# Four hand-written orders of turns, changed in the first stage and in layers 2 and 3

## The chip, the cores and the metric

The kernel runs on one core of one Trainium2 chip. Its time is the device time of one execution in microseconds (us), the median of several runs. The profile adds one more execution, taken by the hardware profiler.

The engines of the core work side by side, each through its own list of instructions in order: TensorE (PE; its weight loads are PEld) multiplies matrices and transposes, VectorE (DVE), ScalarE (ACT) and GpSimd (POOL) do elementwise work, and SyncE (SP) issues the transfers. They meet only through semaphores: an instruction that waits holds up everything behind it on its own engine.

## The reference, cut to what matters

Four layers run on 4 elements of 1024 rows of 128 numbers. Each layer normalises, scales and shifts its input by a row of a modulation, applies a sequence operation, adds it back through a gate, normalises again and applies a feed-forward.

```python
mod = (_silu(L0_c) @ L0_wmod).reshape(L0_c.shape[0], 6, 1, -1)
h = _layernorm(x, axis=-1) * (1 + ca) + sa
x = x + ga * _L0_attn_ref(h, ...)      # relu features, state decayed by gamma, divided by a sum
h = _layernorm(x, axis=-1) * (1 + cb) + sb
x = x + gb * _L0_ffn_ref(h, ...)       # 8 experts, the best 2 of each row
...                                     # layer 1: four small transformer blocks, then 8 experts
...                                     # layer 2: a chunked delta rule, see below
...                                     # layer 3: a gated delta rule along 512 rows
```

The sequence operation of layer 2 needs the inverse of a unit triangular matrix for each chunk and then runs a recurrence over the chunks:

```python
A = solve_triangular(M, jnp.broadcast_to(eye, M.shape), lower=True, unit_diagonal=True)
v = A @ v
k_cumdecay = A @ (k_beta * decay_exp)
def step(S, inp):
    k_i, v_i, kcd_i = inp
    attn = jnp.tril(jnp.einsum('bhid,bhjd->bhij', k_i, k_i) * L[None])
    v_new = v_i - kcd_i @ S
    o_i = k_i * de @ S + attn @ v_new
    S_new = chunk_total_decay * S + jnp.einsum('bhcd,bhce->bhde', k_i * dw, v_new)
```

Layer 3 is of the same family: queries, keys, values, two sigmoids and a gate, a state that is updated at every row, and then a feed-forward of one expert for each part of the batch. The kernel computes it in chunks too, with an inverse and a recurrence.

## The kernel before, in words

Every one of the 4 elements has its own space (`room[b]`, tensor `arena`) and its own two banks of PSUM; small constants lie in `sm`, `cst`, `cols` and `rows`.

For each engine and each element there is a generator: `element_pe`, `element_act`, `element_dve` and `element_pool`, with one more, `common_...`, for what belongs to no element (the decay tables, the biases, the fold of weights). A generator issues the instructions of its engine for its element, layer by layer: `l0_...` and `mods_...`, `moe0_...`, `fold_...`, `l1_...`, `moe1_...`, `l2_...`, `l2f_...`, `l3_...`, `l3f_...`. It yields at many places. What it issues between two yields is here called a turn: often some four matmuls and their waits, one normalisation, or one group of GpSimd's operations. Some turns issue nothing.

Which generator moves next is written out by hand in the dict `TURNS`: a long string of digits for each engine. A digit 0 to 3 gives a turn to that element, 4 to the common part:

```python
parts = [element(b) for b in range(B)] + [common()]
for b in TURNS[h.name]:
    step(parts[int(b)])
for part in parts:
    while step(part):
        pass
```

The strings therefore set how the elements' work is interleaved on each engine, and nothing else. Within one element each engine's order is always the same. Which instruction waits for which is also always the same, with one exception: an element's products alternate between its two banks (`Banks.take`), and a product waits until the reader of that bank has freed it.

SyncE has no string. Its queue is written out in `queue_first` and the functions after it. It loads the inputs, the first weights, then waits in `queue_mods(0)` for the marks "shift" and "gates", that is for VectorE's last step of the first modulation, writes the modulation to DRAM and reads it back for each element (`kept`). Behind that wait stand the small weights, the constants, the experts' weights, the long row `rows` (2253 KB), the fold and the projections of layer 1; two more waits, for "bias3" and "fold", stand before the weights `wf1`, `wf2` and the modulations of layers 2 and 3.

The first stage: `common_act` copies the modulation rows and takes the sigmoid of the decay, `common_dve` makes the decay tables (a scan), adds 1 to the gates and later prepares the biases with `bias_middle` and eight memsets. For each element GpSimd and VectorE take the statistics of the rows (BATCH_NORM_STATS2), ScalarE normalises, TensorE transposes, ScalarE shifts by the modulation while it evicts the bank, and TensorE makes q, k and v; ScalarE applies relu to q and k.

Layer 2 and layer 3: seven rounds of two halves build the inverse on TensorE (`inv_pe`; turns `inv_f` and `inv_p`, the second of which transposes), with evictions by ScalarE and VectorE (`inv_act`, `inv_dve`), and with GpSimd, which shifts, masks and scales columns (`inv_pool`, `shift_pool`, `unit_pool`). The recurrence follows (`d2v` makes the new values, `d2s` the state; `r3...` in layer 3). It passes from TensorE to VectorE or ScalarE and back in each of its steps.

Lines that every operation comes through, and by which the profile names it: L87 matmul, L90 transpose, L98 and L99 ScalarE's activation, L104 elementwise on two tensors, L107 with a scalar, L110 scalar and tensor, L113 copy, L116 memset, L130 and L133 statistics, L136 reciprocal, L147 reduction, L152 a transfer.

## The time and the profile before

| | us |
|---|---|
| median of 3 runs | 1735.24 (1734.53 to 1736.05) |
| profiled execution, its own time | 1735.68 |
| its span, first to last instruction | 1733.9 |
| TensorE busy | 1698.8 (98%) |
| TensorE's weight loads, beside it | 1302.2 (75%) |
| VectorE busy | 1235.9 (71%) |
| GpSimd busy | 1218.6 (70%) |
| ScalarE busy | 1089.0 (63%) |
| number of instructions | 31801 |

Times in the trace run from the start of the span. A row of a timeline gives the start, the duration, the engine and line, the operation with what it writes and reads, and in brackets how long the engine was idle before it and which engine's operation released it. Neighbouring operations of a kind are joined in one row (x4). The granted clock of TensorE is 1.00 of full speed nearly everywhere, so the clock plays no part. In the page's 40 slices TensorE is at 9 tenths or more in all but the first and the last.

### The profile page before, as it was taken

Reading aid. Unit: us, or ns where it says so; the run is one execution under the profiler, and the core shown is the slowest. Engines: PE = TensorE matmul, PEld = TensorE weight load, DVE = VectorE, ACT = ScalarE, POOL = GpSimd, SP = SyncE. Lnnn points to the kernel's source line nnn. Section 1 sums busy time; section 2 is a strip of 40 time slices with the busy share of each in tenths; the row PEclk is TensorE's granted clock in tenths of the full one; section 3 lists DMA queues with packets and bytes.
Section 4 is the critical chain, followed back from the end, with each engine's and each line's share of the span. In section 5 each row is a group of like instructions: output and inputs, shape, how many; then the busy total and the mean of one; then the engine's idle time right before and its main releaser. Section 6 shows DMA issues by size and latency. Waiting matters only on the chain.

```text
span 1733.9 us, 31801 instructions
## 1 busy us (share of the span) xinstructions
PE 1698.8 (98%) x10006; PEld 1302.2 (75%) x10006; DVE 1235.9 (71%) x4490; ACT 1089.0 (63%) x2904; POOL 1218.6 (70%) x1771
## 2 busy tenths in 40 slices
PE   8999999999999999999999999999999899999998
PEld 5888888876667676676676777767788787788976
DVE  7954335688977988988899866445566766578773
ACT  6555226456677678777777886546546666665656
POOL 5655549898878987888799785135347876666667
PEclk9999999999999999999999999999999999999999
DMA  7100000010000000000000000000000001000002
GB/s 254 68 32 1 1 1 4 3 51 1 1 1 1 1 1 1 1 1 1 1 1 1 1 11 6 1 1 7 2 3 3 1 18 31 21 2 1 2 3 73
DMA packets 24027, 26.70 MB, mean 15 GB/s; under 512 B 3492, under 2 KB 20772, under 8 KB 23476
## 3 DMA queue, kind: packets, MB, share of 16 engines
q1 hardware_dynamic: 23860, 24.67, 4.6%
q8 instruction: 81, 1.33, 0.3%
q14 instruction: 86, 0.70, 0.1%
HBM read 22.52 MB, written 2.15 MB: 14 GB/s over the span
## 4 chain that ended last, share of the span: by engine, by line
PE 84%; DVE 5%; POOL 5%; ACT 4%; issue 2%; POOLq 0%; DVEq 0%; ACTq 0%
PE ps L87 77%; PE ps L90 7%; POOL arena L104 5%; ACT arena L98 3%; DVE arena L104 2%; DVE arena L110 1%; DVE arena L147 1%; DVE arena L130 0%; ACT arena L99 0%; ACT L98 0%; DVE arena L133 0%; DVE arena L107 0%; DVE arena L136 0%; DVE ps L147 0%; DVE ps L104 0%
## 5 line engine op out<-in xcount | busy, mean ns | idle before, releaser
L104 POOL TENSOR_TENSOR arena<-arena 128x512 f32<-128x512 f32 (+6 forms) x836 | 715.4, 869 | 277.7 <-DVE arena L110 96.5
L98 ACT ACTIVATE arena<-ps 128x128 f32<-128x128 f32 (+11 forms) x1204 | 338.8, 326 | 393.5 <-PE ps L87 285.2
L87 PE MATMUL ps<-arena 128*128 128x128 f32 (+4 forms) x2792 | 440.5, 291 | 9.1 <-DVE arena L104 3.8
L87 PEld LDWEIGHTS ps<-arena 128*128 128x128 f32 x2792 | 373.4, 192 | 96.0 <-issue 47.6
L104 DVE TENSOR_TENSOR arena<-ps,arena 128x128 f32<-128x128 f32 (+4 forms) x696 | 313.2, 469 | 175.7 <-PE ps L87 163.4
L98 ACT ACTIVATE arena<-arena 128x128 f32<-128x128 f32 (+1 forms) x836 | 321.2, 439 | 50.9 <-POOL arena L104 38.9
L87 PE MATMUL ps<-arena,moe 128*128 128x256 f32 (+1 forms) x960 | 288.2, 439 | 0.0
L87 PE MATMUL ps<-arena,cst 128*128 128x504 f32 (+2 forms) x768 | 283.8, 489 | 2.4 <-ACT arena L98 1.3
L98 ACT ACTIVATE arena<-ps,cols 128x512 f32<-128x512 f32 x324 | 216.8, 688 | 103.2 <-PE ps L87 96.3
L104 POOL TENSOR_TENSOR arena<-arena,cst 128x144 f32<-128x144 f32 (+7 forms) x536 | 186.2, 356 | 92.4 <-ACT arena L98 57.7
L110 DVE SCALAR_TENSOR_TENSOR arena<-ps,arena 128x128 f32<-128x128 f32 (+1 forms) x476 | 157.0, 365 | 119.6 <-PE ps L87 94.1
L90 PE MATMUL ps<-cst,arena 128*128 128x128 f32 (+1 forms) x1296 | 231.4, 274 | 8.6 <-ACT arena L98 6.0
L87 PEld LDWEIGHTS ps<-moe,arena 128*128 128x128 f32 x1728 | 202.2, 192 | 21.7 <-issue 15.0
L104 POOL TENSOR_TENSOR arena<-arena,mhalf 128x4 f32<-128x4 f32 (+1 forms) x140 | 150.3, 1074 | 93.7 <-DVE arena L147 89.5
L87 PEld LDWEIGHTS ps<-arena,moe 128*128 128x128 f32 x960 | 172.7, 191 | 50.9 <-issue 25.0
L90 PEld LDWEIGHTS ps<-cst,arena 128*128 128x128 f32 (+1 forms) x1296 | 157.7, 142 | 67.0 <-issue 24.6
L87 PE MATMUL ps<-moe,arena 128*128 128x128 f32 x1728 | 204.8, 276 | 0.1
L87 PEld LDWEIGHTS ps<-arena,cst 128*128 128x128 f32 x768 | 133.1, 190 | 78.3 <-issue 38.6
L147 DVE TENSOR_REDUCE arena<-arena 128x4 f32<-128x8 f32 (+3 forms) x368 | 180.2, 519 | 16.2 <-POOL arena L104 10.6
L104 POOL TENSOR_TENSOR arena<-arena,rows 128x512 f32<-128x512 f32 (+1 forms) x132 | 141.3, 1072 | 24.4 <-PE ps L90 15.8
L130 DVE BATCH_NORM_STATS2 arena<-arena 128x6 f32<-128x128 f32 x544 | 141.7, 275 | 20.9 <-POOL arena L104 12.8
L87 PE MATMUL ps<-arena,wf 128*128 128x512 f32 x256 | 127.8, 597 | 0.5 <-ACT arena L98 0.4
(120 smaller groups left out, 1761.9 us busy)
## 6 DMA issues: line engine op xcount, KB each, us to landing
rows<-in_rows SPq DMA_DIRECT2D x1, 2253.0 KB, 14.5
arena<-in_x SPq DMA_DIRECT2D x8, 256.0 KB, 5.2
wf<-in_wf SPq DMA_DIRECT2D x2, 1024.0 KB, 7.0
arena<-in_L_ffn_W SPq DMA_DIRECT2D x8, 256.0 KB, 3.0
out_dram<-arena SPq DMA_DIRECT2D x8, 256.0 KB, 2.7
wmod<-in_wmod SPq DMA_DIRECT2D x4, 384.0 KB, 8.1
arena<-kept SPq DMA_DIRECT2D x24, 64.0 KB, 3.0
arena<-kept SPq DMA_DIRECT2D x8, 192.0 KB, 3.2
```

What stands on the lines that cost most here:

```text
L87: return UNSENT if self.e is None else self.e.matmul(out, lhsT, rhs, start=start, stop=stop)
L90: return UNSENT if self.e is None else self.e.transpose(out, in_, ident)
L98: return self.e.activation(out, in_, func, bias=bias, scale=scale)
L104: return UNSENT if self.e is None else self.e.tensor_tensor(out, a, c, op)
L110: return UNSENT if self.e is None else self.e.scalar_tensor_tensor(out, a, s, c, op0, op1)
L130: return UNSENT if self.e is None else self.e.bn_stats(out, a)
L147: return self.e.tensor_reduce(out, a, AX.X, ALU.add, negate=negate)
```

## The change

Only the four strings in `TURNS` change. No function, no instruction, no wait and no buffer is added or taken away; every engine issues what it issued before, in another order.

```diff
--- before.py
+++ after.py
@@ -389,113 +389,113 @@
 TURNS = {
-    "pe": ("2000000000000120002230001222000112200011100211012003013211003031110332001332322330320113213131222121"
-          "1333222011133020000112103211133320042330100300213103322000203332002200300100003001200100032022202021"
-          "0011000230032021022113112213312210002232011011312222110311031101122101101011221210112122011311311221"
...
-          "0122321322331234313231223232000020230232331113111031333120002121120221332023311133231010322033320002"
-          "220333312232322223333133000110211"),
-    "dve": ("4000000000000000440111424242222222001122222230011133303233401000031221110020200113121003111000422202"
-           "3300133330211001112000003131211321300000121111032000033233321212230033331142102122000030030032330120"
-           "0000100011133232223231112110000101102113222000000333330112121320113333210123331221213311101110324211"
...
-           "1111111111111111232112301120032031222222222222222322011000311311113222233323333333333333334411330330"
-           "2222222312330333333213211000200033012141132240201333322233231"),
-    "act": ("4040400040220211222221111030110333333430112204000331000010100010203200210333012020011020222002320200"
...
-           "333222023030220132002220013213333033211023311"),
-    "pool": ("2041004201200302200102003031110011132200403312210012103330202231023133121132033111122133000000012223"
...
-            "10333221102033234012321001133221223233331000111223112122233000132333330011223200"),
+    "pe": ("0400000000002023000212020012200101210001210201021130110031000211130333200132312302333232113123121110"
+          "2233322201113022000111300321314332120013030300330210300032103322200220030010000330012001100020222020"
+          "2001100023003202100221133112213122100223201101131222211031103110112210110101122112011212201131131122"
...
+          "2132321323133231232223000020232203331011310131131332220221102103130113331023023113202233302233223322"
+          "330"),
+    "dve": ("4000000000001440202121200030211244222222132410332022103213012112001000211100010301400213004033321030"
+          "0003223313221131102102201000113110000101131310002320013313233222230303331210242003201120030330030000"
+          "0210100011132331224221312121230020110110132010030000321313230133330123011231313121113302222110311131"
...
+          "1101111111112112323122101130103222222222212222220233101010312013111022323332333333333333332223331032"
+          "1213220333333323232000332213231"),
+    "act": ("0420144400002022212121011100303333334211123203000001300410101200030022201033301020011100222200232020"
...
+          "003332222203331"),
+    "pool": ("4200301422100001200200310100132202110230431332011000233101220323011213111322301313301122000402003213"
...
+          "02031130220331221001223131223233331100001232122333"),
```

In all each string is 30 digits shorter (3333 to 3303 for TensorE, 3861 to 3831 for VectorE, 2145 to 2115 for ScalarE, 1180 to 1150 for GpSimd). Those 30 are turns that issue nothing, and with them the strings between look different in places although they give the same order. Read through the generators, so that only turns that issue something are counted (number 0 is the first), this is what changes:

| engine | working turns | changed at the start | changed behind |
|---|---|---|---|
| TensorE | 2753 | 15 to 114 (53 moved) | 1873 to 2748 (571 moved, by at most 11) |
| VectorE | 3322 | 12 to 252 (190 moved, by at most 18) | 2471 to 3320 (573 moved, by at most 18) |
| ScalarE | 1840 | 1 to 54 (20 moved) | 1301 to 1835 (350 moved, by at most 9) |
| GpSimd | 1030 | 0 to 64 (45 moved) | 715 to 1014 (150 moved, by at most 6) |

TensorE's working turn 115 starts at 92 us in the trace of before, its turn 1873 at 1323.6 us. Behind 1323 us lie layer 2, its feed-forward, layer 3 and its feed-forward, with the four elements interleaved and somewhat apart.

Some of the moves, with the number of the working turn before and after:

- ScalarE: the normalisations of element 0's first half 2 to 1, the first modulation row's copy 1 to 2, the sigmoid of the decay 7 to 4, the second copy of the biases 36 to 44.
- VectorE: the modulation's gates 26 to 42, its step for the shift 22 to 31, the statistics of elements 1, 2 and 3 to places ahead of element 0's last ones, element 0's second half 34 to 44, the decay table of layer 2 55 to 73, the block with `bias_middle` and the memsets 145 to 148, a step of element 1's recurrence 149 to 154.
- TensorE in layer 2: element 3's inverse, round 1, 1957 to 1960 and 1963 to 1966, its round 2 1964 to 1968 and 1971 to 1975, element 1's `d2v` 1982 to 1986, element 0's `d2s` 1991 to 1995, element 3's round 5 stays at 1999.
- TensorE in the last feed-forward: element 1's `f3wo` 2719 to 2722. The last turns of all engines stay as they are.

## Rows read from the trace of the kernel before

**Rows 1.** The page: its span, and the busy time of each engine.
```profile
span 1733.9 us, 31801 instructions
...
PE 1698.8 (98%) x10006; PEld 1302.2 (75%) x10006; DVE 1235.9 (71%) x4490; ACT 1089.0 (63%) x2904; POOL 1218.6 (70%) x1771
```

**Rows 2.** The page: the chain that ended last, by engine.
```profile
PE 84%; DVE 5%; POOL 5%; ACT 4%; issue 2%; POOLq 0%; DVEq 0%; ACTq 0%
```

**Rows 3.** Stretches: length; PE, PEld, DVE, ACT, POOL busy (records); clock; DMA; GB/s.
```profile
0.00:20.00 20.00, 15.50 (x40) 6.66 (x40) 10.79 (x65) 10.06 (x21) 7.64 (x24) 1.00 0.66 161
20.00:92.00 72.00, 70.37 (x473) 57.22 (x474) 64.52 (x336) 40.87 (x68) 47.11 (x71) 1.00 0.41 158
92.00:1323.00 1231.00, 1223.39 (x6672) 907.33 (x6671) 876.20 (x3019) 778.74 (x1922) 873.30 (x1006) 1.00 0.02 4
1323.00:1342.00 19.00, 18.76 (x162) 18.18 (x161) 15.55 (x57) 12.37 (x54) 16.55 (x43) 1.00 0.02 6
1342.00:1372.00 30.00, 25.71 (x199) 22.86 (x198) 21.01 (x67) 18.54 (x83) 25.98 (x71) 1.00 0.00 1
1372.00:1405.00 33.00, 31.38 (x249) 28.02 (x248) 24.27 (x87) 23.38 (x94) 29.08 (x82) 1.00 0.07 19
1405.00:1600.00 195.00, 191.30 (x1353) 159.98 (x1352) 136.40 (x526) 123.64 (x427) 129.23 (x297) 1.00 0.05 13
1600.00:1667.00 67.00, 66.27 (x514) 59.70 (x513) 50.19 (x171) 39.76 (x158) 42.23 (x123) 1.00 0.01 1
1667.00:1691.00 24.00, 19.45 (x132) 15.32 (x131) 20.71 (x116) 15.65 (x38) 16.04 (x30) 1.00 0.03 7
1691.00:1728.50 37.50, 36.36 (x225) 26.86 (x226) 15.56 (x54) 26.03 (x45) 31.44 (x28) 1.00 0.23 61
```

**Rows 4.** Timeline of ScalarE, 5 to 24 us: start, duration, operation.
```profile
9.87 1.63 ACT L98 ACTIVATE arena<-arena 128x128 f32<-128x128 f32 x4
...
16.43 1.28 ACT L98 ACT_TABLE_LOAD   x1
17.73 0.20 ACT L98 ACTIVATE gd<-rows 128x1 f32<-128x1 f32 x1
```

**Rows 5.** Timeline of TensorE, 5 to 23 us.
```profile
11.60 1.09 PE L90 MATMUL ps<-cst,arena 128*128 128x128 f32 x4 [0.87 <-ACT arena L98]
...
18.56 0.49 PE L87 MATMUL ps<-w,arena 128*128 128x128 f32 x2 [0.68 <-ACT arena L98]
```

**Rows 6.** Timeline of VectorE, 48 to 60 us: its longest operation there.
```profile
52.44 1.75 DVE L104 TENSOR_TENSOR wf<-wf,rows 64x1536 f32<-64x1536 f32 x1
```

**Rows 7.** Timeline of TensorE, 55 to 59 us.
```profile
57.40 1.13 PE L87 MATMUL ps<-arena,w 128*128 128x512 f32 x2 [1.05 <-DVE arena L110]
```

**Rows 8.** Timeline of SyncE, 0 to 60 us: two of the transfers issued.
```profile
13.60 0.34 SPq L152 DMA_DIRECT2D kept<-mods  x1
...
23.48 0.46 SPq L152 DMA_DIRECT2D rows<-in_rows  x1
```

**Rows 9.** The page, transfers: count, size, us from issue to landing.
```profile
rows<-in_rows SPq DMA_DIRECT2D x1, 2253.0 KB, 14.5
```

**Rows 10.** Timeline of GpSimd, 36 to 60 us.
```profile
39.63 0.46 POOL L104 TENSOR_TENSOR arena<-arena 128x128 f32<-128x128 f32 x1 [1.24 <-DVE arena L110]
...
42.08 1.46 POOL L113 CAST wf<-rows 128x1536 bf16<-128x1536 f32 x1
...
52.49 2.02 POOL L104 TENSOR_TENSOR arena<-arena 128x128 f32<-128x128 f32 x1 [0.26 <-DVE arena L110]
```

**Rows 11.** Timeline of TensorE, 1350 to 1372 us.
```profile
1353.63 0.41 PE L90 MATMUL ps<-cst,arena 128*128 128x128 f32 x2 [0.56 <-ACT arena L98]
...
1371.57 0.60 PE L87 MATMUL ps<-arena 128*128 128x128 f32 x3 [0.81 <-POOL arena L104]
```

**Rows 12.** Timeline of GpSimd, 1342 to 1372 us: two shifts.
```profile
1352.09 2.62 POOL L104 TENSOR_TENSOR arena<-arena 128x512 f32<-128x512 f32 x2 [0.33 <-ACT arena L98]
```

**Rows 13.** Timeline of TensorE, 1695 to 1698 us.
```profile
1696.81 0.91 PE L87 MATMUL ps<-sm,arena 128*128 128x128 f32 x6 [1.06 <-ACT arena L98]
```

More of the change, by code:

```diff
@@ new lines @@
+    "pool": ("4200301422100001200200310100132202110230431332011000233101220323011213111322301313301122000402003213"
+          "2321200331200300002003033000002211221112222111110000111111011222222033200111112111122321111312003333"
+          "1102023322100001303103322033011100123322003332230230302222103322201020133133233012331012302123001021"
+          "2021333323113212302033122310003213111323030012333012302203213003233011120213311000222133212213303211"
+          "3301203122013210012130201321233213011102320003123300103222120330111213000112330231001003122201221012"
+          "2010313002011233303222133210012132200113201132203301023122232110311123303130213003133222031320220110"
+          "0203102302102200333203312110231221321123200111213002203320102000100031111311111131222222332322223223"
+          "0031003333300133333331333332211100000002000020220011110110312222031102230010032211223112211322322000"
+          "1201002103303010031003123302303233233013311013101221201123112023221123121232232211333213313301332033"
+          "3302033223310313100010030002001023002211100303131112110011010132122133130022322332320013233221213232"
+          "3133021210010323310220003322001203011301210121301011222301122321120123123332212330213232201133303333"
+          "02031130220331221001223131223233331100001232122333"),
```

176 lines of the change are left out of this document (83 added, 93 removed).

## The prediction

> **What bounds the kernel now.** I read the page's busy shares first, then its chain, then busy time by stretch, then the timelines of the stretches where TensorE idles. TensorE is busy for 1698.8 of 1733.9 us [rows 1] and 84% of the chain that ends last lies on it [rows 2]. It does the same work in any order, so a new order can only win back TensorE's idle time and the shorter holes that the pipeline's drain covers. The table by stretch [rows 3] shows where these are. Between 92 and 1323 us TensorE idles 1231.00 - 1223.39 = 7.6 us in 1231: that is where no working turn moves. The changed stretches hold the rest: 4.5 us of idle time in 0 to 20, 1.6 in 20 to 92, 4.3 in 1342 to 1372, 1.6 in 1372 to 1405, 3.7 in 1405 to 1600, 0.7 in 1600 to 1667, 4.6 in 1667 to 1691, 1.1 in 1691 to 1728.5, and a tail of 5.5 us after TensorE's last turn (VectorE's last add and the store), whose last turns stay in order on every engine.
>
> Idle time understates the loss. In 1323 to 1342 TensorE is hardly ever idle and takes 19.00 / 162 = 0.117 us for a matmul record. At that pace the 199 records of 1342 to 1372 need 23.3 us, not 30.0, the 249 of 1372 to 1405 29.2 and not 33.0, and the 132 of 1667 to 1691 15.5 and not 24.0. So these three lose about 6.7, 3.8 and 8.5 us [rows 3]. With the idle time of the others this makes 24.5 us behind 1323 us and some 6 ahead of 92 us: all that any order could give.
>
> **The method for the sum.** I walked both strings through the generators, dropped the turns that issue nothing, and laid the two orders side by side with the old trace. For each hole of TensorE I asked whether the turn that waited comes later in the new order, and how much work of other turns, whose inputs the old trace shows finished at that moment, stands ahead of it now. A hole is filled by the smaller of the two. This uses old finishing times for the inputs; the other engines' turns move too, so it is a first guess and no more.
>
> **First stage, 0 to 92 us.** Four moves matter. (a) ScalarE's four normalisations of element 0 now stand ahead of the copy of the first modulation row. They ran at 9.87 [rows 4] only because that copy waited for TensorE; VectorE and GpSimd had their inputs ready before 7 us. TensorE's first transposes, at 11.60 after 0.87 of idle time [rows 5], can start at 10.7. (b) The sigmoid of the decay, with its table load of 1.28 us and 0.20 for itself [rows 4], moves from ahead of the k activation to ahead of the first shift. It starts at about 11.3 and ends at 12.7, so the shift, at 12.73 before, doesn't gain from (a), and the q product stays at 13.56. The k activation, at 17.84 before, may start when TensorE ends the k product, about 17.3: 0.5 gained. (c) VectorE takes statistics of elements 1 and 2 ahead of the last ones of element 0. These wait for inputs that land by 9.6 and 11.4, so element 0's second half is ready at 13.4 instead of 9.5, and its last normalisation at 17.5 instead of 14.84. The second transposes, at 17.13 before, slip by 0.4; the next products, at 18.56 [rows 5], come at 18.1 all the same. Net 0.4 gained. (d) VectorE's long bias step (1.75 us [rows 6] and eight memsets) goes three turns later, and the three operations of element 1 that stood ahead of element 2's release of a bank (0.65 us) go behind it. The hole of 1.05 before TensorE's turn at 57.40 [rows 7] shrinks by as much. Sum 1.0 us gained. Bounds: 2.6 gained (the whole 1.6 idle of 20 to 92 and (a) to (c) kept), 2 lost, for what (c) does to the queue: the last modulation step, which the sync queue waits for at 13.60 [rows 8], comes 16 turns later, by my count of the turns ahead of it at 17.1. Everything queued behind it slips 3.6 us: the gates, the small weights, the constants, the experts' weights and the long row load, issued at 23.48 [rows 8] and, with 14.5 us to landing [rows 9], there at 38.0, which GpSimd's block that begins with a copy of it asks for at 42.08 [rows 10]. At 41.6 it is just in time; I charge nothing for it, and up to 2 us if it slips more. The late store of the biases (74 instead of 62 us) delays weights that are first used far behind.
>
> On the 1.28 us: ScalarE's next operation starts 1.30 us after the load began [rows 4], and no further wait is in the trace. The Trainium skill, in "ScalarE: Activation LUTs", section "What ACT_TABLE_LOAD costs", adds a drain of about 1.38 us to each switch; by it move (b) would be worth 1.4 us more if it took the load off the chain for good. The trace doesn't bear it out here. The order of functions that need a load is the same in both kernels, so their number (95) stays.
>
> **Layer 2, 1323 to 1405 us.** The largest holes lie in 1342 to 1372: 0.56 at 1353.63, two more like it of 0.56 and 0.46, and 0.81 at 1371.57 [rows 11]. The first is before a turn of element 3's inverse, which goes 3 turns later, with element 2's recurrence and element 0's inverse ahead of it; others like it at 1355.5, 1356.5 and 1359.2 go 3 or 4 turns later. The second and third go 4 turns later, the fourth stays. By the method 2.6 of the 4.3 us idle are filled in 1342 to 1372 and 0.4 in 1372 to 1405. What speaks against it is GpSimd: it is busy 25.98 of the 30.00 us [rows 3], the chain runs on it from 1351.9 to 1371.5 with 2.62 us for two of its widest operations [rows 12], and its own order changes by one or two turns. TensorE can only work ahead on what GpSimd has released. I take 2.5 us, between 0 (GpSimd holds all of it) and 6 (the drains go too).
>
> **The rest of layers 2 and 3, 1405 to 1691 us.** The holes here are short and many, most under 0.5 us. Of the 15.9 us idle time behind 1323, 8.8 stand before turns that now come later, 4.5 before turns that stay, 3.0 before turns that come earlier. By the method 1.2 us are filled in 1405 to 1600, nothing in 1600 to 1667, 1.0 in 1667 to 1691; with the drains that go along (about 0.17 us a hole: my reading of single holes) some 3. Against this stand new holes: of 314 TensorE turns that come earlier from 1323 on, 90 would by the old times not have their inputs. Most of these had their producer moved up as well. I charge 0.5 us. Net 2.5, from 2 lost to 7 gained. In 1667 to 1691 element 3's recurrence alone sets the pace, each of its steps waiting for VectorE or ScalarE, and its TensorE order hardly moves; that caps the gain there.
>
> **The last feed-forward, 1691 to 1734 us.** Of its 1.1 us idle the hole of 1.06 at 1696.81 [rows 13] is before a turn that goes 3 later, with element 2's transposes ahead. 0.7 gained, 0 to 1.2. The final turns are the same.
>
> **Sum.** 1.0 + 2.5 + 2.5 + 0.7 = 6.7 us. The profiled execution took 1735.68 (span 1733.9 and 1.8 around it), 0.44 over the median of 1735.24; against the median this gives 1728.5.
>
> **The rivals.** (1) The forecast: holes filled about as counted, 1719 to 1731.7. Chance 0.62. (2) The holes only change place. In layer 2 GpSimd's work has to be done before the same TensorE turns whatever their order, and near 1680 the recurrence does the same; then only the first stage and the last feed-forward gain, about 1.5 us: 1733.7, between 1731.7 and 1738.7. For it speaks GpSimd's share in 1342 to 1372 [rows 3]; against it that GpSimd is busy only 129.23 of the 195.00 us behind 1405 [rows 3], so there is work to trade. Chance 0.19. Here belongs contention: a 128x128 operation of GpSimd that takes 0.46 us elsewhere took 2.02 [rows 10] beside VectorE's 1.75 us operation on two SBUF tensors [rows 6]; new pairs could cost or spare 1.6 us each. The Trainium skill, "SBUF — State Buffer", section "Who interferes with whom", calls this an exclusive lock of a shared port pair for the whole instruction, and the trace agrees. (3) Slower. In 1600 to 1667 TensorE idles 0.7 us in 67, so a new order can gain nothing and only lose there; by the old times 15 of the 50 turns that come earlier in that region lack their input at their new place, by 8.1 us together. If ScalarE, VectorE and GpSimd don't deliver earlier, each of these becomes a hole, each hole delays the producers of the next, and the loss in this region and the same in 1405 to 1600 passes the gain of 6.7 from about half of the lags on (14.2 and 8.1 us, half of which is 11): 1739.5 and up, to 1746. Against it: producers moved too. Chance 0.14. (4) The gain feeds itself, since a filled hole lets the producers of the next start earlier, and most of the 24.5 us counted above goes: 1710 to 1719. Chance 0.05. That the change isn't what it says I exclude: between TensorE's working turns 115 and 1872 the order is the same on all engines, although digits differ there, which only shift turns without work.
>
> **Numbers.** Faster by over 0.2% (3.5 us, about what a measurement of this kernel can tell from no change): 0.62 + 0.05 = 0.67. Within: 0.19. Slower: 0.14. The range leaves out (4) and the upper half of (3): 1718 to 1739.
>
> **What would show it.** In the profile after: TensorE's start of the first transposes near 10.7 and the products of 18.56 near 18.1; the row load issued near 27 and GpSimd's 8.5 us block still near 42; TensorE's idle time in the stretch that answers to 1342 to 1372 down from 4.3 to about 2; the stretch that answers to 1405 to 1667 no more idle than before; the span from 92 to 1323 as long as before to within 1 us. Wrong if that middle stretch changes by more, if the load comes too late for GpSimd, or if the idle time of layer 3 grows by what layer 2 gives.

## The result, and the profile after

The changed kernel is slower. Its median is 1741.91 us (8 runs, 1740.45 to 1742.24) against 1736.04 us for the kernel before on the same chip (8 runs, 1733.92 to 1737.66), a ratio of 1.0034 (95% interval 1.0025 to 1.0043), some 5.9 us. The prediction had 6.7 us of gain (1728.5, between 1718 and 1739). The profiled execution took 1741.93 us.

The page of the changed kernel, its span and busy times, answers to [rows 1]: 6.2 us more span, TensorE 6.0 us busier though it issues the same 10006 matmul records.

```profile
span 1740.1 us, 31800 instructions
...
PE 1704.8 (98%) x10006; PEld 1303.5 (75%) x10006; DVE 1233.0 (71%) x4490; ACT 1090.3 (63%) x2904; POOL 1221.5 (70%) x1771
```

Its chain by engine answers to [rows 2]: GpSimd has one point more, ScalarE two less.

```profile
PE 84%; POOL 6%; DVE 5%; ACT 2%; issue 2%; DMA 0%; SPq 0%; POOLq 0%; DVEq 0%; ACTq 0%
```

The stretches of [rows 3], same columns, in the changed kernel:

```profile
0.00:20.00 20.00, 14.17 (x39) 5.98 (x40) 11.26 (x68) 9.33 (x18) 7.30 (x27) 0.74 0.55 146
20.00:92.00 72.00, 70.06 (x473) 57.24 (x473) 62.77 (x323) 41.64 (x69) 45.98 (x67) 1.00 0.43 159
92.00:1323.00 1231.00, 1223.28 (x6663) 905.48 (x6663) 877.10 (x3026) 779.91 (x1922) 874.72 (x1005) 1.00 0.02 5
1323.00:1342.00 19.00, 18.89 (x162) 18.00 (x161) 15.06 (x56) 11.29 (x49) 16.03 (x44) 1.00 0.02 6
1342.00:1372.00 30.00, 26.67 (x205) 23.35 (x204) 20.32 (x64) 19.51 (x90) 26.51 (x70) 1.00 0.00 1
1372.00:1405.00 33.00, 31.41 (x246) 27.73 (x245) 24.88 (x92) 22.32 (x88) 29.49 (x86) 1.00 0.01 3
1405.00:1600.00 195.00, 192.76 (x1354) 160.25 (x1353) 135.29 (x523) 123.49 (x431) 130.45 (x296) 1.00 0.06 16
1600.00:1667.00 67.00, 66.65 (x505) 58.73 (x505) 48.54 (x166) 40.48 (x162) 43.36 (x126) 1.00 0.01 1
1667.00:1691.00 24.00, 20.07 (x143) 16.63 (x142) 20.95 (x114) 13.59 (x32) 15.13 (x28) 1.00 0.00 1
1691.00:1728.50 37.50, 35.96 (x202) 26.14 (x201) 14.88 (x64) 27.06 (x50) 27.46 (x27) 0.91 0.19 49
```

Two things stand out. Behind 1323 us TensorE idles less than before in every stretch up to 1691 (0.11, 3.33, 1.59, 2.24, 0.35 and 3.93 us against 0.24, 4.29, 1.62, 3.70, 0.73 and 4.55), and yet the kernel isn't faster. And the granted clock is 0.74 in the first and 0.91 in the last of these stretches.

Such a table can't say where time is lost, since the kernels drift apart under its fixed edges. Both traces have 10006 matmul records, so the n-th of one can be held against the n-th of the other. This is how much later the record comes that starts at the given time in the kernel before (us); it is called the lag below. The other rows are experiments told below: in `s_...` and `after_ctl` the engines' orders are put together from pieces of the old and the new one. The last two columns are the span's end against 1733.9, and that less the lag at 1676:

```
kernel      92      1323    1405    1600    1676    end     tail alone
after      +1.14   +1.44   +1.41   +1.43   +2.54   +6.2    +3.66
after_ctl  +0.78   +0.91   +0.85   +0.86   +1.94   +5.8    +3.86
s_first    +0.97   +0.98   +0.99   +0.66   +0.62   +0.6    -0.02
s_rest     -0.56   -0.57   -0.67   -0.64   +0.44   +3.0    +2.56
s_l23      -1.74   -1.52   -1.53   -1.51   -1.51   -0.1    +1.41
s_l3       +0.70   +0.69   +0.70   +0.39   +1.46   +3.0    +1.54
s_tail     +0.19   +0.47   +0.54   +0.27   +0.24   +2.8    +2.56
s_nottail  +1.52   +1.54   +1.44   +1.47   +2.58   +2.9    +0.32
```

The middle, where no working turn moved, passes the lag on to within 0.3 us, as forecast. 1323 to 1600 us, where the prediction had 3.7 us of gain, gives 0.0 against this one trace of the kernel before; the traces of experiments with the old order there pass it in 0.0 to 0.3 us less, so that 0.2 us are rather lost in it. 1600 to 1676 us costs 1.1 every time that it is new, and the end 2.6 or more with the whole of the new tail.

**The start.** Timeline of TensorE in the changed kernel, where [rows 5] were:

```profile
7.16 0.81 PE L87 MATMUL ps<-wmod,sil 128*4 128x384 f32 x2
10.64 1.44 PE L87 MATMUL ps<-wmod,sil 128*4 128x384 f32 x2 [2.67 <-DVE mcols L107]
...
14.84 3.78 PE L87 MATMUL ps<-arena,w 128*128 128x512 f32 x4 [1.71 <-ACT arena L98]
```

and of VectorE:

```profile
9.34 0.29 DVE L130 BATCH_NORM_STATS2 arena<-arena 128x6 f32<-128x128 f32 x1 [1.67 <-DMA arena<-in_x]
...
10.43 0.16 DVE L107 TENSOR_SCALAR mcols<-ps 128x8 f32<-128x8 f32 x1
```

TensorE's second row product, at 9.24 before, waits 2.67 us for a bank. The bank is freed by VectorE's step that copies the modulation's columns (`mcols`), and that step now stands behind element 1's first statistics, which wait for element 1's rows to land at 9.34.

**The end.** Timeline of GpSimd in the changed kernel from 1700 us:

```profile
1703.48 15.01 POOL L104 TENSOR_TENSOR arena<-arena 128x512 f32<-128x512 f32 x12 [2.94 <-DVE arena L110]
1718.82 14.99 POOL L104 TENSOR_TENSOR arena<-arena 128x512 f32<-128x512 f32 x12 [0.33 <-DVE arena L110]
```

and in the kernel before:

```profile
1698.47 29.94 POOL L104 TENSOR_TENSOR arena<-arena 128x512 f32<-128x512 f32 x24 [0.98 <-DVE arena L110]
```

GpSimd ends both kernels with 24 operations in a row, 1.25 us apart (called its last block below). Before, they run without a pause from 1698.5 to 1728.4. Their start waits for the first expert's biases, which VectorE makes (the mark `f3bor`, L110), and these for TensorE's product with the output weights (`f3wo`), the turn with the hole of [rows 13]. Now they start 5.0 us later, 2.5 more than the lag at 1676. The last transfers, 1730 us to the end in the changed kernel and 1725 us to the end in the kernel before (count, size, us to landing):

```profile
out_dram<-arena SPq DMA_DIRECT2D x5, 256.0 KB, 3.2
```

```profile
out_dram<-arena SPq DMA_DIRECT2D x3, 256.0 KB, 2.6
```

Of the eight stores of the output five are issued after 1732.9 us, around GpSimd's last operation (it ends at 1733.8), and not three, as before after 1727.7 us (there it ends at 1728.4). From GpSimd's last operation to the end of the span it is 6.3 us, not 5.5.

**The clock.** Windows of the changed kernel; then one of the kernel before:

```profile
10.00:19.00 9.00, 6.65 (x13) 2.75 (x14) 8.12 (x52) 4.82 (x9) 4.49 (x9) 0.50 0.35 84
20.00:24.00 4.00, 3.29 (x19) 2.23 (x19) 3.12 (x16) 3.65 (x9) 2.07 (x4) 1.00 0.76 140
1685.00:1691.00 6.00, 4.59 (x34) 3.65 (x35) 5.00 (x33) 5.89 (x15) 3.17 (x5) 1.00 0.00 0
1693.00:1698.00 5.00, 4.62 (x16) 3.14 (x16) 3.48 (x23) 4.16 (x7) 0.94 (x2) 0.50 0.39 97
```

```profile
1685.00:1691.00 6.00, 4.02 (x26) 2.71 (x25) 5.30 (x35) 5.17 (x14) 2.72 (x4) 1.00 0.10 22
```

TensorE's longest hole in the 6 us ahead of 1692.2, in the changed kernel:

```profile
1688.89 0.66 PE L90 MATMUL ps<-cst,arena 128*128 128x128 f32 x4 [0.48 <-ACT arena L98]
```

TensorE ran at 1.2 GHz (0.50) from 9.4 to 19.6 and from 1692.2 to 1699.0 us. [rows 3] say 1.00 for the first 20 us of the kernel before, but the records of its clock only begin at 17.4: ahead of them, at 13.56 us, four 512-column records take 3.78 us, just as in the changed kernel at 0.50, and at 1693.82 four take 1.93. So the clock was low in both starts, and what was said ahead of the prediction, that it plays no part, doesn't hold for them. In the tail it is a difference of the two executions.

### The profile page after: what moved, and what is told of

It is laid out like the page before. It is cut to its first block, busy times and chain, and to the rows that moved or that the text cites. A ratio compares the mean times of both kernels' runs of the same rounds, so it can differ in the third digit from the quotient of the medians.

```text
span 1740.1 us, 31800 instructions
## 1 busy us (share of the span) xinstructions
PE 1704.8 (98%) x10006; PEld 1303.5 (75%) x10006; DVE 1233.0 (71%) x4490; ACT 1090.3 (63%) x2904; POOL 1221.5 (70%) x1771
## 4 chain that ended last, share of the span: by engine, by line
PE 84%; POOL 6%; DVE 5%; ACT 2%; issue 2%; DMA 0%; SPq 0%; POOLq 0%; DVEq 0%; ACTq 0%
PE ps L87 77%; PE ps L90 7%; POOL arena L104 5%; DVE arena L104 2%; ACT arena L98 2%; DVE arena L110 1%; DVE arena L147 1%; DVE arena L130 1%; DMA arena<-in_x 0%; DVE arena L133 0%; SPq L152 0%; DVE arena L107 0%; ACT L98 0%; POOL wf L104 0%; DVE ps L147 0%
## 5 line engine op out<-in xcount | busy, mean ns | idle before, releaser
L98 ACT ACTIVATE arena<-ps 128x128 f32<-128x128 f32 (+12 forms) x1204 | 339.8, 326 | 406.7 <-PE ps L87 291.9
L87 PE MATMUL ps<-arena 128*128 128x128 f32 (+3 forms) x2792 | 446.5, 292 | 8.3 <-DVE arena L104 2.8
L90 PE MATMUL ps<-cst,arena 128*128 128x128 f32 (+1 forms) x1296 | 237.3, 276 | 6.8 <-ACT arena L98 2.6
L110 DVE SCALAR_TENSOR_TENSOR arena<-ps,arena 128x128 f32<-128x128 f32 (+1 forms) x476 | 156.9, 364 | 113.8 <-PE ps L87 87.5
```

Of the source, the lines that this page charges most:

```text
L87: return UNSENT if self.e is None else self.e.matmul(out, lhsT, rhs, start=start, stop=stop)
L90: return UNSENT if self.e is None else self.e.transpose(out, in_, ident)
L98: return self.e.activation(out, in_, func, bias=bias, scale=scale)
L110: return UNSENT if self.e is None else self.e.scalar_tensor_tensor(out, a, s, c, op0, op1)
```

## The experiments

The strings were cut where, on each engine, old and new order have done the same turns; one piece is then taken from the old and another from the new order. The cuts, as working turns of TensorE, VectorE, ScalarE and GpSimd: at 700 us (983, 1327, 635, 411), 1405 us (2089, 2632, 1445, 784), 1600 us (2488, 3042, 1691, 933) and 1676 us (2687, 3219, 1791, 1011). Ratios are to the kernel before, on the chip of the run, of 5 to 11 runs (m_nopool 4).

**The whole again (after_ctl)** is the changed kernel itself.

> The whole change once more, on the chip of its fellows of this call, for the sum. By the traces the parts are: first stage +1.9 us (mean of three new against seven old first stages), 1323 to 1600 us 0.0, 1600 to 1676 us +1.1, tail +2.6, together 5.6 us over before (1.0032), with a mean granted clock of 0.994 to 0.996. If the parts measured alone add up by their medians it is 8 us (1.0046).

1.0037 (1.0024 to 1.0051), 6.4 us, with a clock of 0.994 in three of five runs. Both sums, 5.6 by the traces and 8 by the medians, lie within the interval of 4.2 to 8.8 us, so this run doesn't decide between them.

**One part new: s_first, s_rest, s_l23, s_l3, s_tail; all but one: s_nottail.**

```diff
 # pieces:      to 700   to 1405   to 1600   to 1676   to the end
+# s_first      new      old       old       old       old
+# s_rest       old      new       new       new       new
+# s_l23        old      new       new       old       old
+# s_l3         old      old       old       new       old
+# s_tail       old      old       old       old       new
+# s_nottail    new      new       new       new       old
```

> The new order up to 92 us on all four engines, the old order behind. In the trace of the changed kernel TensorE's turn at 92 us comes 1.14 us later than before. If the first stage's loss stands by itself and is carried to the end, this kernel takes 1.2 us more than before (ratio 1.0007) and its mean granted clock is a little lower. Rival: the middle absorbs it, since the transfers and the other engines have slack there: 0.0. Rival: the later stage only suffers because the elements arrive with other distances: 6 us more here too.

1.0022 (1.0013 to 1.0032), 3.8 us; the profiled execution was the fastest of the ten and shows 0.97 us at 92 us. Over all traces of this case, four new first stages stand at +1.10 us at 92 us in the mean (0.78 to 1.52) and ten old ones at -0.88 (-1.85 to +0.70): 2.0 us. The loss is there and is passed on; that its size is 3.8 by the median and 2.0 by the traces stays open.

Part of the 2.0 goes with the clock. The clock's records show 1.2 GHz for 3.4, 6.8 or 10.2 us of the first 25 in these traces (that of the kernel before has none ahead of 17.4). Old starts with 3.4 us of it stand at -1.39 to -1.85 at 92 us (m_nopool, g_new, t_wo, g_before), with 6.8 at -1.74 and -0.56 (s_l23, s_rest), with 10.2 at -0.86, +0.19 and +0.70 (t_store, s_tail, s_l3). New starts stand at +0.78 with 6.8 (after_ctl) and at +0.97, +1.14 and +1.52 with 10.2. At the same length of low clock the new first stage is therefore 1.2 us late (10.2) or 1.9 (6.8), and not all of that can be laid to the order by single traces.

> The old order up to 1323 us, the new one behind. If the parts add up, this is 6.2 - 1.4 = 4.8 us over before (ratio 1.0028), with the same fall of the clock near 1692 us and GpSimd's last block of 24 operations starting some 3.8 us late. If the two parts work only together, it is within 1 us of before.

1.0024 (1.0014 to 1.0034), 4.2 us. The parts are independent, or nearly: nothing in the later stages needs the first one's shift to go wrong. GpSimd's last block starts at 1700.23, 1.8 us late and not the expected 3.8.

> The turns from 1323 to 1600 us are new, the first stage and everything behind 1600 us old. Of the 5 us that the prediction expected from this stretch the trace of the changed kernel shows nothing: lag 1.44 at 1323 and 1.43 at 1600. Theory: no gain and no loss, 0.0 (0.9990 to 1.0010). Rival: the gain is there and is eaten by the first stage's shift, then 2 to 5 us under before.

0.9999 (0.9990 to 1.0008). No gain, no loss, and the table of lags says 0.0 between 1323 and 1600 us too.

> Only the turns from 1600 to 1676 us are new. In the trace of the changed kernel TensorE's lag grows from 1.43 to 2.54 us in this stretch. If that stands by itself, this kernel is 1.1 us over before (1.0006), and if the old tail can't take it up GpSimd's block starts as much later. Rival: it is absorbed by the waits of the tail, 0.0. The clock stays at full speed here if the fall near 1692 us belongs to the tail's order.

1.0010 (1.0001 to 1.0019), and 1.07 us in the trace between 1600 and 1676. That is 1.7 us by the median. The expectation on the clock failed: it fell at 1681.9 in this trace, with the old tail. So the fall doesn't belong to the new tail.

> Only the turns behind 1676 us are new (the end of layer 3 and the last feed-forward). Theory: GpSimd's last 24 operations of 1.25 us run without a pause before, and may start only when VectorE has made the biases of the first expert. In the new order that step stands behind three steps of element 2 which wait for TensorE's router product, and TensorE's product for it stands 3 turns later. So GpSimd's block starts some 2.5 us later and the kernel ends 2.5 to 3.5 us later (ratio 1.0014 to 1.0020). Rival: the tail is harmless and was only pushed by layer 3, then 0.0 to 0.5 us. Rival: the loss is the half clock near 1692 us; then the trace shows it fall and the q of the rows (0.27 us a 128-column product) go to 0.42 for 3.4 to 6.8 us.

1.0014 (1.0005 to 1.0023), 2.4 us; the clock stayed up in the trace and the tail costs 2.56 us all the same. GpSimd's block starts 1.3 us later than the lag at 1676 gives, and not the expected 2.5, and the last 1.2 us come after its start, in the pause between its halves and behind it:

```profile
1700.05 15.02 POOL L104 TENSOR_TENSOR arena<-arena 128x512 f32<-128x512 f32 x12 [2.59 <-DVE arena L110]
1715.40 15.02 POOL L104 TENSOR_TENSOR arena<-arena 128x512 f32<-128x512 f32 x12 [0.33 <-DVE arena L110]
```

> Everything new except the turns behind 1676 us. If the parts add up: 3.7 (first stage, as measured by itself) + 1.1 = 4.8 us over before less what the old tail absorbs, and 2.5 to 3.5 us below what the whole change costs on the same chip; as the whole change costs 5.9 (4.3 to 7.5), this gives 2.5 to 4.8 us over (1.0014 to 1.0028). If the tail is harmless it costs as much as the whole change.

1.0022 (1.0013 to 1.0031), 3.8 us, inside the expected 2.5 to 4.8. With the old tail the block runs through and the tail alone costs 0.3.

**The first stage: f_mcols, fm, f_fill, f_dve, b_fill.** In f_mcols (everything new) and fm (new to 700 us, old behind) one of VectorE's turns goes back:

```diff
 # VectorE's working turns from 11 on, element:step
 0:stats
-1:stats
 common:dec0
 common:mcols
+1:stats
 0:stats
```

> The changed kernel with one turn of VectorE put back: element 1's first statistics stand behind the step that copies the modulation columns (and so frees the bank for TensorE's second row product). If VectorE's wait for element 1's rows, which land at 9.34 us, is what holds that product up, TensorE's hole of 2.67 us at 8.0 goes, the shift starts before 13.4 and TensorE is some 1.2 to 2 us earlier at 92 us than in the changed kernel: 4 to 5 us over before. Rival: the hole moves to the next wait (ScalarE's table load and the late second half of element 0), gain under 0.5 us.

1.0035 (1.0022 to 1.0049). In the trace TensorE is 1.75 us earlier at 92 us than in the changed kernel, as expected, at the same 10.2 us of low clock. The median is not: it is 6.1 us over before (3.8 to 8.5), where 4 to 5 were expected and the changed kernel has 5.9. Five runs can't tell 2 us, but a turn that cost over 3 us should have shown. So it was tried on the part alone:

> New order up to 92 us on all engines with the one turn of VectorE put back (element 1's first statistics behind the copy of the modulation's columns), old order behind. The new first stage alone is 3.7 us over before (2.3 to 5.5) and 1.9 by the traces. Theory: that one turn is the cost of the first stage; with it back the first stage is 0 to 1 us over before, and TensorE's hole at 8.0 is gone. Rival: the rest of the new first stage costs too (the late second half of element 0 and the late release of the sync queue): 2 us or more over.

1.0003 (0.9994 to 1.0012), 0.5 us (1.0 under to 2.1 over), where the first stage with that turn in its new place costs 3.8 (2.3 to 5.5). By these two medians that one turn is the cost of the first stage; how much it costs stays between the 1.75 us of the traces and the 3.3 of the medians. The prediction's point (c) shows too, TensorE in this kernel:

```profile
9.07 0.81 PE L87 MATMUL ps<-wmod,sil 128*4 128x384 f32 x2 [0.52 <-DVE mcols L107]
...
17.15 1.09 PE L90 MATMUL ps<-cst,arena 128*128 128x128 f32 x4 [1.88 <-DVE arena L107]
```

The second transposes wait 1.88 us for VectorE's late last normalisation, and start at 17.15, as before at 17.13.

```diff
 # f_fill: the changed kernel; mods_pe, ahead of the second row product
+if l == 0 and h == 1:
+    for _ in range(12):
+        pe.mm(banks.tiles[B - 1][1][:, :], warm[:, 0:128], warm)
```

> The changed kernel with twelve idle products of the warming kind put into TensorE's hole of 2.67 us before the second row product. They cost nothing while TensorE waits and keep it busy. If the clock that fell to half from 9.4 to 19.6 us is what makes the first stage late, the q and k products take 0.59 us a piece and not 1.06, and TensorE is 1.5 us or more earlier at 92 us. If the wait itself is all, the time is as in the changed kernel, to within 0.3 us (ratio 1.0035).

1.0037 (1.0024 to 1.0051). The clock stayed up until 14.4 us and fell then for 3.4 us, and TensorE waited 2.17 us for ScalarE's shift instead; the q and k products still took 3.58 us. The median didn't move. In the trace TensorE was at +0.27 us at 92 us and not at 1.10, with the wait for `mcols` in its place: 0.8 us go with the clock, half of what was expected if it were the cause, and 1.2 us against the mean of the old starts stay.

```diff
 # b_fill: the kernel before; 3, 3 and 2 such products ahead of element 0's
 # first transposes, its q product and its first scores
+if b == 0 and g == 0:
+    for _ in range(3):
+        pe.mm(banks.tiles[B - 1][1][:, :], warm[:, 0:128], warm)
```

> The kernel before with eight more idle products of the warming kind, three ahead of element 0's first transposes, three ahead of its q product and two ahead of its first scores, where TensorE waits 0.87, 0.87 and 0.68 us. If the half clock in the first 20 us costs what the records say (a 512-column product 1.06 and not 0.59 us), a clock held up by these is worth 1 to 2 us: 0.9988 to 0.9995 of before, and a version faster than both. Rival: at half clock they take 0.43 us each and delay the transposes themselves: 0 to 1 us slower.

0.9997 (0.9988 to 1.0006). The clock was low from 9.5 to 12.95 us only, the q and k products took 1.98 us and not 3.78, and at 92 us TensorE stood at -0.39, inside the spread of the ten old starts. There is no version here that is clearly faster than both.

```diff
 # f_dve: to 700 us
-TensorE old, VectorE old, ScalarE old, GpSimd old
+TensorE old, VectorE new, ScalarE old, GpSimd old
```

> Only VectorE's order up to 92 us is new, the other three engines old. The new first stage on all four costs 3.7 us (2.3 to 5.5). Theory: VectorE's wait for element 1's rows ahead of the modulation's columns is the cost, so that this kernel shows TensorE's hole before the second row product and is 2 to 4 us over before. Rival: the hole only shows because ScalarE's order changed with it, or ScalarE's own order costs: within 1 us of before.

1.0052 (1.0038 to 1.0065), 9 us: more than the whole change. TensorE's lag is 0.6 us at 18.8 and 8.2 at 92: one engine's new order against three old ones loses at many places. This kernel says little on the turn in question. It says that VectorE's new order doesn't go with the other three old ones.

**GpSimd in layer 2: m_nopool, g_before, g_new.**

```diff
 # m_nopool: 1323 to 1676 us, all else old
-TensorE old, VectorE old, ScalarE old, GpSimd old
+TensorE new, VectorE new, ScalarE new, GpSimd old
```

> From 1323 to 1676 us TensorE, VectorE and ScalarE new, GpSimd old; everything else old. In all kernels with the new order here TensorE's lag stays at 0.0 from 1323 to 1600 us and grows by 1.1 us from 1600 to 1676. If GpSimd's new order is what takes the gain of layer 2 away, the lag falls by 1 to 3 us up to 1600. If it is the orders of the other three, the same 0.0 and +1.1 come out. If GpSimd's order was made to fit the others, taking it away costs: lag over +2 us at 1676.

1.0118 (1.0103 to 1.0134). The third case: +3.4 us by 1405, +10.8 more by 1600, +3.7 more by 1676. GpSimd's turns move by at most 6 places, and without these moves the other three orders cost 20 us by the median, 18 by the trace. Other mixtures of old and new engines in this stretch were not run.

```diff
 # g_before, and g_new with the new order from 1323 to 1600 us (shift_pool)
-pool.tt(four(m.h), four(m.h), over(r.row(1)), ALU.mult).then_inc(*pool.up(b))
-pool.wait_ge(*pool.last(b))
-pool.tt(four(m.h), four(m.h), over(r.row(0)), ALU.add).then_inc(*pool.up(b, "d2h", b, g))
+pool.tt(four(m.h), four(m.h), over(r.row(1)), ALU.mult).then_inc(*pool.up(b, "d2h", b, g))
```

> The kernel before with GpSimd's second operation of each shift of layer 2 left out (the addition of the shift row; eight operations of 1.28 us). The output of layer 2 lacks that row. If GpSimd sets the pace from 1342 to 1405 us, TensorE's lag falls by 2 to 5 us over layer 2. Rival: TensorE with its short waits sets it: under 1 us.

> The same work left out of GpSimd's shifts in layer 2, with the new order from 1323 to 1600 us and the old one elsewhere. If GpSimd's share is what kept the filled holes of layer 2 from shortening it, the new order gains over the old one here, 1 to 3 us at 1600 us. If short waits for the other engines took the place of the holes whatever GpSimd does, the two are equal to 0.3 us, as they are with the full work (0.0).

One execution each. Of 10.2 us of work taken from GpSimd the old order gives 1.2 us back between 1323 and 1600 (lag -1.76 to -2.95), the new one 0.5 (-1.28 to -1.75); traces of one order differ by up to 0.3 us in this stretch. So GpSimd bounds a small part of layer 2 in the old order, less of it in the new one, and its work isn't what eats the filled holes: with a lighter GpSimd the new order stands 0.7 us worse, not better.

**The tail: t_store and t_wo**, both s_tail with something put back.

```diff
 # t_store: VectorE's last turns
 2:f3x/0
+1:f3x/1
 0:f3x/1
 3:f3x/0
 2:f3x/1
-1:f3x/1
 3:f3x/1
```

> The kernel with only the tail new (behind 1676 us), and in it VectorE's add of element 1's second half put back from the last but one place to where it was, 3 turns earlier. SyncE issues the stores in the order of the elements, so in the new tail the store of element 1 and the four of elements 2 and 3 behind it wait for that add. Theory: with the add back, SyncE issues element 1's store near 1722, only three stores are left behind VectorE's last adds, and the time from GpSimd's last operation to the end of the span falls from 6.3 to 5.5 us as before, some 1 us less than with the tail alone (2.9 us over before at the median). Rival: the stores at the end overlap anyway: no change in that time.

1.0007 (0.9998 to 1.0016) against 1.0014 (1.0005 to 1.0023): by the medians the two can't be told apart. In the trace GpSimd's last operation to the end of the span takes 5.2 us (6.3 in s_tail), and the tail alone costs 1.35 and not 2.56 us. The last transfers, from 1725 us on, of s_tail and then of this kernel:

```profile
out_dram<-arena SPq DMA_DIRECT2D x5, 256.0 KB, 3.2
```

```profile
out_dram<-arena SPq DMA_DIRECT2D x3, 256.0 KB, 2.6
```

> The kernel with only the tail new, and in it three stretches put back: ten turns of TensorE, seven of VectorE and eighteen of ScalarE around the first experts' products and biases (f31, f3wo, f3w2o, the first gelus against element 2's features). The late store stays. Theory: GpSimd's block of 24 starts at the lag of 1676 us plus 0 to 0.3 and not 1.3 us later, and the kernel is some 1.5 us faster than with the tail alone: 0.5 to 1.5 us over before, what is left being the stores. Rival: GpSimd's block doesn't bound the end, TensorE does: then the block starts early and pauses, and the time is within 0.5 us of the tail alone.

1.0019 (1.0010 to 1.0028), not faster than s_tail, and in the trace the tail alone costs 3.1 us. The rival had it right on the block, which starts earlier and pauses; the time is 0.5 (traces) to 0.9 us (medians) over s_tail, a little more than it said:

```profile
1697.24 15.00 POOL L104 TENSOR_TENSOR arena<-arena 128x512 f32<-128x512 f32 x12 [2.14 <-DVE arena L110]
1713.56 15.00 POOL L104 TENSOR_TENSOR arena<-arena 128x512 f32<-128x512 f32 x12 [1.31 <-DVE arena L110]
```

The block starts 0.5 us nearer to its old place and then pauses 1.31 us, waiting for element 2's `f3bor`. TensorE's `f3wo` for element 2 comes after 0.49 us of idle time behind ScalarE's gelu in this kernel as in the changed one. ScalarE's second copy of element 2's transposed features stands 6 turns later than before in both; that this is the cause is not shown. Which of the tail's remaining moves is to blame was not taken apart further.

**Is the account complete? (two_turns)**

```diff
 # the changed kernel with
+VectorE's 1:stats back behind mcols, and its 1:f3x/1 back
+the turns from 1600 to 1676 us old
```

> The changed kernel with what the runs so far charge taken out: VectorE's turn with element 1's first statistics back behind the modulation's columns (3.3 to 3.6 us), VectorE's add of element 1's second half back (1.1 to 1.5 us), and the turns from 1600 to 1676 us old (1.1 to 1.7 us). New stay the first stage, 1323 to 1600 us and the tail. If the account is complete, what is left is the later start and the pause of GpSimd's last block, 1.4 us over before (1.0005 to 1.0012). If something is missing from it, it is 3 us over or more.

1.0013 (1.0004 to 1.0022), 2.2 us (0.7 to 3.8). Two turns and 76 us of layer 3 put back take away some 4 of the 6 us. What is left is 1.6 by the trace (span 1735.5), which has 6.8 us of low clock in its tail, and 2.2 by the median, neither the expected 1.4 nor the 3 at which something would be missing; the interval holds both.

## Why the prediction was wrong, step by step

By the traces the 5.6 to 6 us are the first stage (2.0, of which up to 0.8 may be the clock), 1600 to 1676 us (1.1), and the tail (2.6), with 0.9 to 1.3 from the clock on top in those executions in which it falls near 1690 us.

- **First stage, predicted 1.0 gained; 2.0 by the traces, 3.8 by the median, lost.** The failed step is (c) together with (a). (c) saw that VectorE takes statistics of elements 1 and 2 ahead of element 0's and that these wait for their rows, with the right landing times (9.6 and 11.4; measured 9.34 and 11.14). It charged that wait to element 0's second half alone. The modulation's columns stand behind the same wait on the same engine, and TensorE's second row product needs their bank. So (a)'s start of the transposes at 10.7 became 12.02, and the products expected at 18.1 came at 19.40. A new wait has to be charged to everything that is queued behind it, banks freed included; fm and the trace of f_mcols, where the transposes start at 10.19, show that it is this turn. (b) was right that the table load goes off the k activation; it then stands at 12.62 ahead of the shift, at 14.02, where the prediction had 12.7. (d), predicted at 0.6 gained, gave nothing to speak of: the hole of 1.05 us at 57.40 went, and TensorE waits 0.83 us at 53.34 and 0.31 at 59.49 instead; the lag is 1.20 at 52.7 us and 1.12 at 60.3. This hole changed its place, as rival (2) has it.
- **The sync queue** slipped by 3.1 us (16.69 against 13.60 in [rows 8]; 3.6 predicted), the row load was issued at 26.52 (27 predicted), and GpSimd's block began at 43.25, no later than TensorE's lag. This step held.
- **Layer 2 and 1405 to 1600, predicted 3.7 gained; 0.0.** The holes went as the method said. TensorE's waits from 1323 to 1405 us, before (engine, line, waited for: us, times, longest):

```profile
PE ps L87 <- POOL arena L104: 1.4, 4, 0.8
PE ps L90 <- ACT arena L98: 1.3, 5, 0.6
PE ps L87 <- DVE arena L104: 1.0, 3, 0.5
PE ps L87 <- ACT arena L98: 0.8, 2, 0.5
PE ps L87 <- DVE arena L110: 0.7, 2, 0.4
PE ps L87 <- DVE arena L107: 0.6, 1, 0.6
PE ps L87 <- POOL arena L113: 0.2, 1, 0.2
```

  and in the changed kernel:

```profile
PE ps L87 <- DVE arena L110: 1.3, 2, 0.9
PE ps L87 <- ACT arena L98: 1.2, 2, 0.9
PE ps L90 <- ACT arena L98: 0.8, 2, 0.4
PE ps L87 <- DVE arena L104: 0.4, 2, 0.3
PE ps L87 <- POOL arena L104: 0.2, 1, 0.2
```

  6.0 us of waits (those of over 0.15 us) became 3.9. But the time from one record's start to the next tells the rest. Against the usual 0.11 us of a 128-column record (0.43 of a 512-column one), the steps that take over 0.3 us more fell from 28 with some 13.8 us to 16 with 8.6 us between 1323 and 1600; those that take 0.03 to 0.3 more rose from some 145 with 13.3 us to 180 with 18.5. All of this growth lies at records that wait for a semaphore (8.0 us before, 13.1 after); the short steps without a wait stay at 5.3 us. So they are waits, and what the filled holes gave, 5.2 us, they took. The profile counts most of them as busy, which is why TensorE's idle time fell and its busy time rose. The failed step is the assumption that a hole's drain goes with it and that new holes cost only 0.5 us; they were looked for in the rival's region and not here.
- **1600 to 1676 us, inside a term of 2.5 gained; 1.1 lost** in every trace that has it new: the short steps rose there from 38 with 3.1 us to 56 with 4.8, the long ones fell from 4 to 3. Rival (3) named this region as the one where a new order can only lose, and the place was right, its price of 8 us too high. Why these steps are longer is not shown.
- **The last feed-forward, predicted 0.7 gained; 2.6 lost.** The hole of [rows 13] was filled by the transposes of element 2, as said. The turn behind that hole starts GpSimd's last block, which the same profile shows at 29.94 us without a pause: putting work ahead of it delays the end by that work. I had taken the stretch as TensorE's because its idle time was all I asked for. [rows 3] has GpSimd at 31.44 of 37.50 us here. And "the final turns are the same" was false for VectorE, where element 1's second add moved from the fifth last to the next to last place. SyncE stores in the order of the elements, so that the stores of elements 2 and 3 wait for it: 1.2 us, by the trace of t_store. The other half, some 1.3 us, is the later start and the pause of GpSimd's block; t_wo moved them against each other and did not take them away, so which of the remaining moves is to blame stays open.
- **The clock** was not in the sum. With the old tail the end alone costs 1.4 to 1.5 us in the traces in which TensorE is at 1.2 GHz for 3.4 us near 1690 (s_l23, s_l3, fm) and 0.0 to 0.9 in those without (s_first, s_nottail and g_new among them). With the new tail 3.4 us of it cost nothing (s_rest, 2.56 as s_tail and f_mcols without it), and 6.8 us 0.9 to 1.3 (f_fill, the changed kernel, after_ctl). It comes in some executions of the same kernel and not in others: the mean clock of the changed kernel is 0.994 in five of eight runs, as in the profiled one, and 0.999 in one, which leaves room for at most some 5 us at 1.2 GHz in all, start included. The kernel before had 0.996 to 1.000 over its runs. In the changed kernel it fell with no hole of TensorE over 0.5 us in the 6 us ahead, and with more work in them (4.59 us) than the kernel before had where it didn't fall (4.02). The Trainium skill, in "TensorE: Matmul & The Clock Gate", section "Why this matters for your kernels", ties such a fall in mid-kernel to a long idle gap; these rows don't agree. What brings it here stays open.

The prediction also gives 15.9 us of idle time behind 1323 where its three parts (8.8, 4.5 and 3.0) and [rows 3] make 16.3; nothing hangs on it. The time landed in the range that rival (3) gave (1739.5 to 1746), with a chance of 0.14, but its mechanism made only 1.1 of the 6 us, so that the number is luck for that rival. Point by point the account of moves was mostly right and the bookkeeping of who stands behind a moved turn was not.

## What to carry to other kernels

Ask of a filled hole who is released by the turn behind it, and of a moved turn who stands behind it on its engine, which buffer it frees and which queue passes it: two turns of the 1950 that moved cost some 3 of the 4.6 us that the traces lose at both ends. Judge an order by record against record, not by idle time, since most short waits count as busy. And orders written for several engines fit each other: new ones for three of four cost 20 us here, and one of four 9 (one mixture of each was run).

## What the runs showed of the hardware

- Short waits hardly show in the busy share: 5.2 us more of them in 277 us of this kernel, with TensorE's idle time down by 2.6 us at the same time.
- TensorE's clock falls to half near 1690 us in some executions of one and the same kernel and was there for 3.4 or 6.8 us in these traces. It went with 0 to 1.5 us at the end of the kernel; why it costs more in one tail than in the other is not shown.
- 512-column records run at 1.2 GHz near 14 us in the kernel before (3.78 us for four, 1.93 later) though its clock rows say nothing of it: its records start with a change at 17.4 us.
- In the first 25 us the low clock lasts 3.4 to 10.2 us in traces of one and the same order, and TensorE is 1.6 us later at 92 us with 10.2 than with 3.4 (means of three and four old starts).
